# Graph attention on one core: the third attention's row products in two halves around a turned scan, and VectorE's values ahead of the next last maxima

## The chip, the cores and the metric

The kernel runs on 1 core of one Trainium2 chip. The metric is the device time of one execution in microseconds. All times below are from that core. Its engines are named as the profile names them: PE is TensorE (PEld its weight loads), DVE is VectorE, ACT is ScalarE, POOL is GpSimd and SP is SyncE.

## What is computed

Four graph layers run one after the other over 5000 nodes and 85000 edges, which are sorted by destination. Each adds its result to the node features:

```python
h = jnp.maximum(_layernorm(x, axis=-1), 0.0)
x = x + _L0_gnn_ref(h, src, dst, ...)      # mean of the neighbours' rows
h = jnp.maximum(_layernorm(x, axis=-1), 0.0)
x = x + _L1_gnn_ref(h, src, dst, ...)      # relu of two products per edge, mean
h = jnp.maximum(_layernorm(x, axis=-1), 0.0)
x = x + _L2_gnn_ref(h, edge_index, ...)    # two GAT attentions, 16 heads of 8
h = jnp.maximum(_layernorm(x, axis=-1), 0.0)
x = x + _L3_gnn_ref(h, edge_index, ...)    # one dot-product attention, 2 heads of 64
```

The three attentions share one form: a logit for each edge and head, its maximum over the edges of a destination, the exponential of the difference, and a weighted sum of the source rows. In the first two (GAT) the logit is `leaky_relu(al_s[src] + al_d[dst])`. In the third it is the dot product of the destination's query row with the source's key row:

```python
alpha = (q[dst] * k[src]).sum(-1) * (1.0 / np.sqrt(C))
m = jax.ops.segment_max(alpha, dst, num_segments=n)
a = jnp.exp(alpha - m[dst])
denom = jax.ops.segment_sum(a, dst, num_segments=n)
agg = jax.ops.segment_sum(a[:, :, None] * v[src], dst, num_segments=n)
```

## The kernel before

Edges lie in tiles of 128, one edge to a partition. Eight tiles (G = 8) make a group, and 88 groups cover all edges. Five passes sweep over the 88 groups: sum, MLP, GAT, GAT, dot; between them short phases update the nodes. The three attentions are one function, `softmax_pass`, with `kind` "gat" (flag `gat`) or "dot".

In a pass every engine has its own program, and counted semaphores (`eng.wait_ge(*name(p.g))`) join them. A call `turn(p)` stands for one step of an engine's loop, and `p.plus(d)` is the group d further on, so one turn works on several groups at once. The order inside `turn` is the order in which the engine works: it goes through its list strictly, and a wait holds up all that stands behind it.

POOL fetches the source rows of each edge with 8 indirect DMAs a group (L1000) into a ring of 4 slots, `GT`. It may refill a slot when `values` of the group that used it is done. In the dot pass a row has 256 floats (key and value), in the GAT passes 144.

What one turn for group p does in the dot pass, before the change:

- PE: `pe_maxima(p)` (L1313, 24 small products) reads what `dve_lastmax(p)` made; `pe_sums(p-2)` (L1334) adds the weighted rows of each node; `pe_logitT(p+1)` (L1297) turns the logits; `pe_maxedge(p)` (L1321, 24 small products) waits for the running maxima `newM`; `pe_segT(p+1)` (L1303) turns the scanned maxima `seg` back and waits for the scan of DVE; `pe_toedge(p+2)` calls `rows_to_edges` (L1018 to L1024), which takes the destination's query row to each edge: 8 float32 products of 128x128, which the trace shows as 16 passes, into `psD`. They need `Ot32`, which ACT casts in `turn_32`, and a list of 8 block numbers that `loaded` (L185) puts into registers of the engine.
- DVE: `dve_prod(p+1)` (L1346) multiplies `psD` with the key rows; `dve_logit(p+1)` (L1355) sums them; `dve_pen`, `dve_tmax`, `dve_max` make the running maxima (L1378 to L1413); `dve_add(p-2)` (L1436, L1440) adds what `pe_sums` made to `acc`; `dve_segmax(p+1)` (L1362) is the scan over the turned logits; `dve_below(p)` (L1418, L1421) subtracts the maximum; `dve_lastmax(p+1)` (L1370, L1372, L1374) needs `pe_segT(p+1)`; `dve_values(p)` (L1427) weighs the value rows with `factors` and needs ACT's exponential.
- ACT: `act_rescale(p)`; `act_empty(p-1)` (L1269) clears the places that `pe_sums` adds into, and waits for `dve_add(p-2)`; `act_weight(p)` (L1275, L1278) makes the exponentials out of `below`; `act_onehot32(p)` (L1237).

The GAT turn has the same form. Its `dve_prod` is L1343, it has a small `toedge` of 24 bfloat16 products (L1290) in place of the row products, DVE begins with `dve_pen(p)`, and `lastmax`, `newM` and the logits are 8 times as wide.

Of the kernel before, what the change touches and what calls it, by code (L numbers as in the profile page):

```python
# [13 lines left out]
G = 8  # L14
# [51 lines left out]
def program(nc, x, src, dst, w0, b0, w_edge, w_node, b_node, w1, as1, ad1, b1, w2, as2, ad2, b2,  # L66
# [4 lines left out]
    NB = -(-N // P)  # L71
# [23 lines left out]
    with ctx:  # L95
# [20 lines left out]
        blk = sb("blk", [1, SP_], I32)  # L116
# [64 lines left out]
        def loaded(eng, which, table, g, n, most, of=None):  # L181
            if (eng.engine, which) not in reg_sets:
                reg_sets[eng.engine, which] = [eng.alloc_register(f"{which}_{j}") for j in range(n)]
            regs = reg_sets[eng.engine, which]
            eng.load(regs, table[0:1, bass.ds(g * (of or n), n)])  # L185
            return [eng.snap(r, min_val=0, max_val=most) for r in regs]
# [828 lines left out]
            eng.wait_ge(*toedge(p.g - 2))  # L1015
            eng.copy(Ot32[:, p.q, :, :], Ot[:, p.k, :, :]).then_inc(turned32.sem, 1)  # L1016

        def rows_to_edges(eng, p, b):  # L1018

            eng.wait_ge(*turned32(p.g))  # L1020
            eng.wait_ge(*prodded(p.g - 1))
            for j in range(G):
                ins = eng.matmul(psD[:, j, :], Ot32[:, p.q, j, :], at_block(nodeQ, b[j], D), start=True, stop=True)  # L1023
            ins.then_inc(toedge.sem, 1)  # L1024

        def load_hots(eng, p, rows_free, turned_free):

# [176 lines left out]
        def softmax_pass(kind, table, h):  # L1204
            gat = kind == "gat"
# [73 lines left out]


            def pe_toedge(eng, p):
                if not gat:
                    rows_to_edges(eng, p, loaded(eng, "blocks", blk, p.g, G, NB - 1))
                    return
                eng.wait_ge(*staged(p.g))
                eng.wait_ge(*ring_hotT[p.k](p.i))
                eng.wait_ge(*prodded(p.g - 1))
                for j in range(G):
                    for part in range(3):
                        ins = eng.matmul(dst_logits[:, j, :], Ot[:, p.k, j, :], stageD[:, p.q, j, part * h:(part + 1) * h],  # L1290
                                         start=part == 0, stop=part == 2)
                ins.then_inc(toedge.sem, 1)
# [31 lines left out]
            def pe_places(eng, p):  # L1324
                return loaded(eng, "places", blk_off, p.g, G, 2 * BANK + STRIDE)
# [116 lines left out]
            with nc.Block() as block:  # L1442
# [36 lines left out]
                @block.tensor  # L1479
                def _(eng):  # L1480
                    def turn(p):
                        if p.has(-2):
                            off = pe_places(eng, p.plus(-2))
                        if p.has(0):
                            pe_maxima(eng, p)
                        if p.has(-2):
                            pe_sums(eng, p.plus(-2), off)
                        if p.has(1):
                            pe_logitT(eng, p.plus(1))
                        if p.has(0):  # L1490
                            pe_maxedge(eng, p)
                        if p.has(1):
                            pe_segT(eng, p.plus(1))
                        if p.has(2):
                            pe_toedge(eng, p.plus(2))
                    sweep(eng, NG, turn, early=2, late=2)

                @block.vector
                def _(eng):
                    tables_stored(eng)  # L1500
                    eng.memset(lastmax[:, :, :, h:h + 1], 0.0)
                    eng.memset(lastmax1[:, :, :, h:h + 1], 0.0)

                    def turn(p):
                        if gat:
                            if p.has(0):
                                dve_pen(eng, p)
                            if p.has(1):
                                dve_prod(eng, p.plus(1))
                            if p.has(0):  # L1510
                                dve_tmax(eng, p)
                            if p.has(1):
                                dve_logit(eng, p.plus(1))
                            if p.has(0):
                                dve_max(eng, p)
                        else:
                            if p.has(1):
                                dve_prod(eng, p.plus(1))
                                dve_logit(eng, p.plus(1))
                            if p.has(0):  # L1520
                                dve_pen(eng, p)
                                dve_tmax(eng, p)
                                dve_max(eng, p)
                        if p.has(-2):
                            dve_add(eng, p.plus(-2))
                        if p.has(1):
                            dve_segmax(eng, p.plus(1))
                        if p.has(0):
                            dve_below(eng, p)
                        if p.has(1):  # L1530
                            dve_lastmax(eng, p.plus(1))
                        if p.has(0):
                            dve_values(eng, p)
                    sweep(eng, NG, turn, early=2, late=2)
            close((index, onehot32, toedge, prodded, logit, logitT, segmax, segT, flagged, lastmaxed,
                   lastmax1ed, lastmax2ed, nmax, pens, tmaxed, resets, carried, forward, newMed, newM1ed, newM2ed, drop, rescale,
# [46 lines left out]
```

## Time and profile before

| | us |
|---|---|
| median of 3 runs | 5167.67 |
| lowest and highest | 5164.42, 5171.92 |
| the profiled execution | 5178.65 |
| its span in the trace | 5176.9 |

| engine | busy us | share of the span |
|---|---|---|
| PE | 3180.1 | 61% |
| PEld | 2813.0 | 54% |
| DVE | 2733.0 | 53% |
| ACT | 2152.4 | 42% |
| POOL | 3365.2 | 65% |

The profiled execution took 11.0 us more than the median. No engine is busy for more than 65% of the span, so the averages don't tell what bounds the kernel. The passes have to be read one by one: how far apart two turns start, which wait comes in each turn, and what ends it.

### The profile page before, as it was taken

Reading aid. Unit: us, or ns where it says so; the run is one execution under the profiler, and the core shown is the slowest. Engines: PE = TensorE matmul, PEld = TensorE weight load, DVE = VectorE, ACT = ScalarE, POOL = GpSimd, SP = SyncE. Lnnn points to the kernel's source line nnn. Section 1 sums busy time; section 2 is a strip of 40 time slices with the busy share of each in tenths; the row PEclk is TensorE's granted clock in tenths of the full one; section 3 lists DMA queues with packets and bytes.
Section 4 is the critical chain, followed back from the end, with each engine's and each line's share of the span. In section 5 each row is a group of like instructions: output and inputs, shape, how many; then the busy total and the mean of one; then the engine's idle time right before and its main releaser. Section 6 shows DMA issues by size and latency. Waiting matters only on the chain. (4 is left out here: it accounts for less than half of the span.)

```text
span 5176.9 us, 111400 instructions
## 1 busy us (share of the span) xinstructions
PE 3180.1 (61%) x29524; PEld 2813.0 (54%) x29525; DVE 2733.0 (53%) x6724; ACT 2152.4 (42%) x6586; POOL 3365.2 (65%) x3551
## 2 busy tenths in 40 slices
PE   1555555566666665666666646666665566666664
PEld 0444444455655654565656536566564466666664
DVE  4222222332222225677777767777777666666666
ACT  2222222243333325666666556666664333333332
POOL 1777777557777772777777537777773366666662
PEclk9766666687777777656666656665666777676766
DMA  4333333233333332444444224444441344444442
GB/s 125 106 105 105 105 105 104 80 101 105 105 105 105 105 97 60 115 117 118 117 113 117 78 83 118 117 113 118 117 117 54 111 141 134 133 132 135 134 133 74
DMA packets 331553, 563.97 MB, mean 109 GB/s; under 512 B 79101, under 2 KB 149773, under 8 KB 331438
## 3 DMA queue, kind: packets, MB, share of 16 engines
q0 software_dynamic: 124288, 289.37, 21.2%
q1 hardware_dynamic: 207170, 273.48, 16.3%
q8 instruction: 42, 0.69, 0.1%
q14 instruction: 53, 0.43, 0.0%
HBM read 490.38 MB, written 72.84 MB: 109 GB/s over the span
## 5 line engine op out<-in xcount | busy, mean ns | idle before, releaser
L1000 POOL DMA_INDIRECT GT<-table,srcI x3520 | 3351.0, 952 | 1688.0 <-issue 1055.0
L1334 PE MATMUL psA<-V,O 128*128 128x144 f32 (+1 forms) x4224 | 932.8, 403 | 17.4 <-ACT psA L1269 14.9
L1334 PEld LDWEIGHTS psA<-V,O 128*128 128x128 f32 x4224 | 864.8, 294 | 24.0 <-issue 18.7
L1023 PE MATMUL psD<-nodeQ,Ot 128*128 x2816 | 608.0, 403 | 386.9 <-ACT Ot L1016 298.8
L1023 PEld LDWEIGHTS psD<-nodeQ,Ot 128*128 128x128 f32 x2816 | 561.6, 305 | 416.0 <-issue 416.0
L1055 DVE TENSOR_TENSOR acc<-acc,psA 128x1032 f32 (+1 forms) x176 | 215.1, 1222 | 703.6 <-PE psA L1134 673.9
L1269 ACT COPY psA<-consts 128x1296 f32<-128x1296 f32 (+1 forms) x264 | 318.6, 1207 | 368.0 <-DVE acc L1440 368.0
L1180 DVE TENSOR_TENSOR prod<-psD,GT 128x1024 f32<-128x1024 f32 x88 | 107.7, 1224 | 667.1 <-DMA GT<-table,srcI 667.1
L1046 PE MATMUL psA<-zerob 1*128 1x258 bf16 (+1 forms) x704 | 164.5, 378 | 414.1 <-issue 329.1
L1258 ACT COPY nodeM<-newM 128x16 f32 x1408 | 307.7, 219 | 259.2 <-ACT nodeM L1258 230.3
L1440 DVE TENSOR_TENSOR acc<-acc,psA 128x1296 f32 (+1 forms) x264 | 385.6, 1461 | 55.4 <-PE psA L1334 26.2
L1303 PE MATMUL psT<-ident,seg 128*128 128x128 f32 (+1 forms) x264 | 95.7, 362 | 470.1 <-DVE seg L1362 470.1
L1010 ACT COPY srcI<-srcT 128x8 int32 (+1 forms) x440 | 84.3, 193 | 689.3 <-DMA GT<-table,srcI 682.1
L1263 ACT ACTIVATE resc<-diff 128x16 f32<-128x16 f32 (+1 forms) x264 | 55.9, 212 | 733.5 <-DVE acc L1436 687.6
L1165 ACT ACTIVATE V<-prod 128x1024 f32<-128x1024 f32 x88 | 93.0, 1057 | 616.4 <-DVE prod L1180 616.4
L1321 PEld LDWEIGHTS psS<-newM,Ot 128*128 128x128 bf16 x6336 | 189.3, 99 | 290.8 <-DVE newM L1413 288.9
L1321 PE MATMUL psS<-newM,Ot 128*128 128x16 bf16 (+1 forms) x6336 | 211.3, 174 | 212.8 <-DVE newM L1413 212.5
L1134 PE MATMUL psA<-GT,O 128*128 128x129 f32 x1408 | 329.8, 427 | 0.0
L1134 PEld LDWEIGHTS psA<-GT,O 128*128 128x128 f32 x1408 | 305.9, 329 | 36.6 <-issue 36.6
L1046 PEld LDWEIGHTS psA<-zerob 1*128 1x128 bf16 x704 | 68.7, 118 | 470.5 <-issue 447.6
L1427 DVE TENSOR_TENSOR V<-GT,psA 128x1024 f32<-128x1024 f32 x264 | 320.8, 1215 | 3.7 <-ACT psA L1275 3.4
L1303 PEld LDWEIGHTS psT<-ident,seg 128*128 128x128 f32 (+1 forms) x264 | 43.4, 164 | 492.1 <-DVE seg L1362 323.0
(221 smaller groups left out, 5304.1 us busy)
## 6 DMA issues: line engine op xcount, KB each, us to landing
Ob<-onehots SPq DMA_DIRECT2D x352, 256.0 KB
Ot<-onehots_turned SPq DMA_DIRECT2D x352, 256.0 KB
GT<-table,srcI POOLq DMA_INDIRECT x3520
onehots<-Ob SPq DMA_DIRECT2D x88, 256.0 KB
onehots_turned<-Ot SPq DMA_DIRECT2D x88, 256.0 KB
first<-first_dram SPq DMA_DIRECT2D x176, 64.0 KB
first_dram<-GT SPq DMA_DIRECT2D x18, 384.0 KB, 5.1
table<-GT SPq DMA_DIRECT2D x40, 144.0 KB, 1.9
```

What stands on the lines that cost most here:

```text
L1000: eng.indirect_dma_start(out=GT[:, p.k, j, 0:table.shape[1]], out_offset=None, in_=table, in_offset=bass.IndirectOffsetOnAxis(ap=srcI[:, p ...
L1023: ins = eng.matmul(psD[:, j, :], Ot32[:, p.q, j, :], at_block(nodeQ, b[j], D), start=True, stop=True)
L1046: eng.matmul(psA[:, a:a + 2, 0:w], zerob[0:1, 0:P], zerob[0:1, 0:2 * w], start=True, stop=False, skip_group_check=True)
L1055: eng.tensor_tensor(a, a, psA[:, :, 0:w], ALU.add).then_inc(added.sem, 1)
L1134: ins = eng.matmul(to, O[:, p.q, j, :], GT[:, p.k, j, 0:w], start=False, stop=j == G - 1, skip_group_check=True)
L1258: eng.copy(at_block(nodeM, b[j], h), by_step(newM[:, p.q, 0:HG])[:, :, j]).then_inc(noted.sem, 1)
L1269: eng.copy(places, consts[:, 0:1, :].unsqueeze(1).to_broadcast([P, 3, 3, VW])).then_inc(emptied.sem, 1)
L1303: eng.transpose(segR, seg[0:HG, p.q, :], ident[0:HG, 0:HG]).then_inc(segT.sem, 1)
L1321: ins = eng.matmul(edge_max[:, j, :], Ot[:, p.k, j, :], part, start=n == 0, stop=n == 2)
L1334: ins = eng.matmul(flatA[:, bass.ds(off[j], VW)], O[:, p.q, j, :], V[:, p.q, j, 0:VW], start=False, stop=j == G - 1, skip_group_check=True)
L1427: eng.tensor_tensor(v[:, :, :, 0:C], heads(GT[:, p.k, :, f0:f0 + D], h), wide(factors, C), ALU.mult)\
L1440: eng.tensor_tensor(to, to, places, ALU.add).then_inc(added.sem, 1)
```

## The change

Two things change, both in the order of one engine's work, and no instruction of computation is added or removed.

In the dot pass alone, PE issues the 8 products of `rows_to_edges` in two halves of 4, one before `pe_segT` and one behind it. The registers with the block numbers are loaded at the start of the turn. In all three attentions, DVE does `dve_values(p)` before `dve_lastmax(p+1)`.

```diff
-        def rows_to_edges(eng, p, b):
-
-            eng.wait_ge(*turned32(p.g))
-            eng.wait_ge(*prodded(p.g - 1))
-            for j in range(G):
+        def rows_to_edges(eng, p, b, half=None):
+
+            if not half:
+                eng.wait_ge(*turned32(p.g))
+                eng.wait_ge(*prodded(p.g - 1))
+            for j in range(G) if half is None else range(half * G // 2, (half + 1) * G // 2):
                 ins = eng.matmul(psD[:, j, :], Ot32[:, p.q, j, :], at_block(nodeQ, b[j], D), start=True, stop=True)
-            ins.then_inc(toedge.sem, 1)
+            if half != 0:
+                ins.then_inc(toedge.sem, 1)
...
                     def turn(p):
                         if p.has(-2):
                             off = pe_places(eng, p.plus(-2))
+                        if not gat and p.has(2):
+                            b = loaded(eng, "blocks", blk, p.g + 2, G, NB - 1)
                         if p.has(0):
                             pe_maxima(eng, p)
...
                             pe_maxedge(eng, p)
+                        if not gat and p.has(2):
+                            rows_to_edges(eng, p.plus(2), b, 0)
                         if p.has(1):
                             pe_segT(eng, p.plus(1))
                         if p.has(2):
-                            pe_toedge(eng, p.plus(2))
+                            if gat:
+                                pe_toedge(eng, p.plus(2))
+                            else:
+                                rows_to_edges(eng, p.plus(2), b, 1)
...
                         if p.has(0):
                             dve_below(eng, p)
+                            dve_values(eng, p)
                         if p.has(1):
                             dve_lastmax(eng, p.plus(1))
-                        if p.has(0):
-                            dve_values(eng, p)
```

PE in the loop of the dot pass, before: from the last product of `pe_maxedge` (L1321) over the turned scan (L1303) and the load of the block numbers (L185) to the row products (L1023).

```order
L1321 MATMUL psS<-newM,Ot 128x2 x24
L1303 MATMUL psT<-ident,seg 128x16
L185 ISA
L185 TENSOR_LOAD blk
L186 ISA
L1021 REGISTER_ALU
L1023 ISA
L1023 MATMUL psD<-nodeQ,Ot 128x128
L1023 ISA
L1023 MATMUL psD<-nodeQ,Ot 128x128
```

The same place after, where L1320 is `pe_maxedge`, L1302 the turned scan and L1024 the row products:

```order
L1320 MATMUL psS<-newM,Ot 128x2 x24
L1021 REGISTER_ALU
L1022 REGISTER_ALU
L1024 ISA
L1024 MATMUL psD<-nodeQ,Ot 128x128
L1024 ISA
L1024 MATMUL psD<-nodeQ,Ot 128x128
L1024 ISA
L1024 MATMUL psD<-nodeQ,Ot 128x128
L1024 ISA
L1024 MATMUL psD<-nodeQ,Ot 128x128
L1302 MATMUL psT<-ident,seg 128x16
```

Four row products now stand ahead of the turned scan, and the load of `blk` is gone from between the scan and the rest of them.

PE at the border of two turns after the change, from the second half's last product to the next `pe_maxima` (L1312):

```order
L1024 MATMUL psD<-nodeQ,Ot 128x128
L185 ISA
L185 TENSOR_LOAD blk_off
L186 ISA
L185 ISA
L185 TENSOR_LOAD blk
L186 ISA
L1312 MATMUL psS<-lastmax,Ob 128x3 x24
```

The load of `blk` now follows that of `blk_off`, which alone stood here before.

DVE in the loop of the GAT passes, before: `dve_below` (L1418, L1421), the three steps of `dve_lastmax`, then `dve_values` (L1427).

```order
L1418 TENSOR_TENSOR below<-lg,psS 128x128 [waits weight,maxedge]
L1421 TENSOR_SCALAR below<-below 128x128 [waits belowed]
L1370 ISA [waits nmax,segT]
L1370 TENSOR_TENSOR lastmax<-psT,lastT 128x8x16
L1372 TENSOR_TENSOR lastmax<-lastmax 128x8x16 [waits lastmaxed]
L1374 TENSOR_TENSOR lastmax<-lastmax 128x8x16 [waits lastmax1ed]
L1427 TENSOR_TENSOR V<-GT,psA 128x128x8 [waits sums,factor]
```

The same place after, one line number lower:

```order
L1417 TENSOR_TENSOR below<-lg,psS 128x128 [waits weight,maxedge]
L1420 TENSOR_SCALAR below<-below 128x128 [waits belowed]
L1426 TENSOR_TENSOR V<-GT,psA 128x128x8 [waits sums,factor]
L1369 ISA [waits nmax,segT]
L1369 TENSOR_TENSOR lastmax<-psT,lastT 128x8x16
L1371 TENSOR_TENSOR lastmax<-lastmax 128x8x16 [waits lastmaxed]
L1373 TENSOR_TENSOR lastmax<-lastmax 128x8x16 [waits lastmax1ed]
```

The values with their wait for ACT's factors now stand directly behind `below`, and the last maxima come behind them. The dot pass has the same move.

## Rows read from the trace of the kernel before

**Rows 1.** Windows inside a GAT and the dot pass: busy time of each engine.

```profile
core 0: us, PE busy (x) PEld busy (x) DVE busy (x) ACT busy (x) POOL busy (x), PEclk, DMA share, GB/s
...
2100.00:2920.00 820.00, 552.12 (x7290) 499.61 (x7290) 592.59 (x1537) 520.84 (x2019) 622.80 (x648) 0.64 0.42 117
...
4110.00:5110.00 1000.00, 667.54 (x6914) 621.71 (x6914) 646.20 (x1610) 326.62 (x840) 642.51 (x678) 0.73 0.44 133
```

**Rows 2.** First and last start of the logits' first step: dot, then first GAT.

```profile
L1346 DVE TENSOR_TENSOR prod<-psD,GT x88: 1223/1225/1225, 4088.9 to 5114.6; 128x1024 f32<-128x1024 f32 x88
...
L1343 DVE TENSOR_TENSOR lg<-psD,GT x88: 290/291/293, 2056.9 to 2939.1; 128x128 f32<-128x128 f32 x88
```

**Rows 3.** Waits of the dot pass, 4110:5110, total, times, longest.

```profile
DVE prod L1346 <- PE psD L1023: 238.6, 84, 3.0
...
POOL GT L1000 <- DVE V L1427: 149.7, 72, 2.4
...
PE psD L1023 <- issue: 85.9, 84, 1.1
```

**Rows 4.** Timeline of one turn of the dot pass: start, duration, engine, line.

```profile
4658.86 0.26 PE L1303 MATMUL psT<-ident,seg 16*128 16x16 f32 x1 [1.95 <-DVE seg L1362]
...
4660.14 3.78 PE L1023 MATMUL psD<-nodeQ,Ot 128*128 x16 [1.03 <-issue]
...
4663.71 0.83 PE L1313 MATMUL psS<-lastmax,Ob 128*128 128x3 bf16 x24
4663.96 1.22 DVE L1346 TENSOR_TENSOR prod<-psD,GT 128x1024 f32<-128x1024 f32 x1 [2.94 <-PE psD L1023]
...
4668.19 0.76 PE L1321 MATMUL psS<-newM,Ot 128*128 128x2 bf16 x24 [1.04 <-DVE newM L1413]
...
4669.11 1.37 DVE L1440 TENSOR_TENSOR acc<-acc,psA 128x1170 f32 x1
...
4670.95 0.20 PE L1303 MATMUL psT<-ident,seg 16*128 16x16 f32 x1 [2.00 <-DVE seg L1362]
4671.31 0.18 DVE L1370 TENSOR_TENSOR lastmax<-psT,lastT 128x16 f32<-128x16 f32 x1 [0.23 <-PE psT L1303]
...
4671.67 0.18 ACT L1275 ACTIVATE psA<-below 128x16 f32<-128x16 f32 x1
4671.74 0.19 DVE L1374 TENSOR_TENSOR lastmax<-lastmax 128x16 bf16<-128x16 f32 x1
```

**Rows 5.** The fetches by line, in a GAT and in the dot window.

```profile
L1000 POOL DMA_INDIRECT GT<-table,srcI x648 | 623.3, 962 | 197.5 <-issue 193.5 <-DVE V L1427 4.0
...
L1000 POOL DMA_INDIRECT GT<-table,srcI x678 | 642.5, 948 | 346.9 <-issue 197.3 <-DVE V L1427 149.7
```

**Rows 6.** Windows for line 1334 (`pe_sums`) alone, GAT and dot: PE busy.

```profile
2100.00:2920.00 820.00, 326.72 (x1296) 303.47 (x1296) 0.64 0.42 117
...
4110.00:5110.00 1000.00, 211.63 (x1344) 194.93 (x1344) 0.73 0.44 133
```

**Rows 7.** Timeline of one turn of the first GAT pass.

```profile
2620.29 0.29 DVE L1370 TENSOR_TENSOR lastmax<-psT,lastT 128x128 f32<-128x128 f32 x1 [0.21 <-PE psT L1303]
...
2620.94 0.29 DVE L1374 TENSOR_TENSOR lastmax<-lastmax 128x128 bf16<-128x128 f32 x1
2621.15 1.21 DVE L1427 TENSOR_TENSOR V<-GT,psA 128x1024 f32<-128x1024 f32 x1
...
2621.49 0.79 PE L1313 MATMUL psS<-lastmax,Ob 128*128 128x17 bf16 x24 [0.72 <-DVE lastmax L1374]
...
2622.13 4.19 PE L1334 MATMUL psA<-V,O 128*128 128x144 f32 x16
...
2624.24 0.29 DVE L1343 TENSOR_TENSOR lg<-psD,GT 128x128 f32<-128x128 f32 x1 [1.76 <-DMA GT<-table,srcI]
...
2627.79 1.50 DVE L1440 TENSOR_TENSOR acc<-acc,psA 128x1296 f32 x1
...
2630.59 0.28 ACT L1275 ACTIVATE psA<-below 128x128 f32<-128x128 f32 x1
```

More of the change, by code:

```diff
@@ L1281, in pe_toedge @@
             def pe_toedge(eng, p):
-                if not gat:
-                    rows_to_edges(eng, p, loaded(eng, "blocks", blk, p.g, G, NB - 1))
-                    return
                 eng.wait_ge(*staged(p.g))
```

## The prediction, made before the changed kernel had run

> **What bounds the kernel now.** I start from the windows of single passes, since the page's shares mix passes with different limits. No engine is full in either of them [rows 1]: in the dot window PE is busy 668 of 1000 us, DVE 646, POOL 643. So each pass is bounded by a cycle of waits or by an issue rate. The starts of one instruction give the length of a turn. In the dot pass 88 of them lie between 4088.9 and 5114.6, which is 1025.7 / 87 = 11.79 us a turn; in the GAT pass it is 882.2 / 87 = 10.14 us [rows 2].
>
> Next the waits, and what ends them. In the dot pass DVE waits once a turn for the row products (238.6 us in 84 turns, 2.84 each), and POOL waits for DVE's values (149.7 us) [rows 3]. So POOL runs ahead until its ring is full, and the pass hangs on a cycle between PE and DVE. One turn shows it [rows 4]: the turned scan starts at 4658.86, the row products follow at 4660.14 after 1.03 us of "issue", they last 3.78 us, and only then `prod` starts (4663.96). From `prod` to the next turned scan it is 4670.95 - 4663.96 = 6.99 us, DVE's own work nearly throughout. The cycle is 1.28 + 3.82 + 6.99 = 12.09 us in this turn, a long one, and has no slack. PE itself stands idle for 2.00 us before the turned scan (1.95 in the turn before) [rows 4].
>
> The GAT passes are different. There DVE's first step waits for the fetched rows (1.76 us in the turn shown [rows 7]), and POOL issues without a stop: its busy time and its gaps make 623.3 + 197.5 = 820.8 us of a window of 820 [rows 1, 5], 81 turns of 10.13 us. POOL's issue is the floor of that pass, and DVE's 1.76 us are the slack that the change may use up.
>
> **Part 1: the row products in two halves.** The first half now lies in PE's idle 2.00 us before the turned scan. Half of 3.78 us is 1.89 us, and the stretch from the end of `maxedge` (4668.19 + 0.76 = 4668.95) to the turned scan (4670.95) is 2.00 us long [rows 4]. It fits with nothing over. What the half waits for (`turned32`, `prodded` of the group before) was done turns or microseconds earlier: that `prod` ended at 4665.18 [rows 4]. The 1.03 us of issue after the turned scan are the load of the block numbers: 85.9 us in 84 turns, the only thing that stands between [rows 3]. It moves behind the second half, next to the load that is already there, where PE has queued products to work on. So from the turned scan to `prod` remain about 0.25 us for the scan itself and 1.89 us for the second half, with 0.04 to 0.1 us of hand-over: 2.2 us where 5.10 stood (4663.96 - 4658.86) [rows 4]. That takes 2.9 us out of PE's side of the cycle, as much as the whole wait of `prod`. The moved load can cost between 0, if it is hidden, and its 1.03 us; I take 0, because today the neighbouring load costs no gap there (the row products end at 4663.92, and `maxima` starts at 4663.71, in their tail) [rows 4].
>
> What is late next? First DVE's own list. `prod` to `add` is 4669.11 - 4663.96 = 5.15 us. `add` to factors, through ACT's clearing, is 4671.67 - 4669.11 = 2.56 us, 0.18 for the factors and some 0.04 to the values. The last maxima take 4671.74 + 0.19 - 4671.31 = 0.62 us [rows 4], and the values 1.21 (from the GAT turn, the same shape [rows 7]). Sum: 5.15 + 2.56 + 0.22 + 1.21 + 0.62 = 9.76 us, and some 0.2 less where neighbours overlap: 9.5 to 9.8. Second, PE's own list: maxima 0.8, sums 211.63 / 84 = 2.52 us in the mean and up to the GAT pass's 4.19 at the lower clock [rows 6, 7], `maxedge` 0.8, two halves of 1.9, turned scan 0.25 and the turned logits about as much: 8.4 to 10.1 us with everything back to back. Third, POOL: 8 fetches of 0.948 us, each with its gap of issue. Over all 678 fetches the gap is 197.3 / 678 = 0.29 us, over the 606 that it is put down to 0.33: 9.91 to 10.19 us a turn; the GAT row's 10.13 lies between [rows 5]. **POOL is the largest**, and I take the middle, 10.05 us. The dot pass then becomes bounded by issue, like the GAT passes: 87 x (11.79 - 10.05) = **151 us saved**, between 139 (at 10.19) and 164 (at 9.91).
>
> **Part 2: values ahead of the last maxima, dot pass.** Before, the last maxima filled the time in which ACT made the factors: the factors are ready at 4671.67 + 0.18 = 4671.85, the maxima end at 4671.93 [rows 4]. The values can start at most 0.1 us earlier, and the last maxima come 1.2 us later. That delay sits inside the 9.5 to 9.8 us above, and is hidden by POOL's 10.05. Cost 0; without that cover it would be 0 to 0.6 us a turn.
>
> **Part 3: the same move in the two GAT passes.** Here there is no gain to have: POOL's issue is the floor. There is a cost, if a longer cycle passes 10.13 us. I follow it [rows 7]. The values start when the factors are ready: `add` starts at 2627.79, factors end at 2630.59 + 0.28 = 2630.87, which makes 3.08 + 0.04 = 3.12 us. The values take 1.21, less 0.08 of overlap. The last maxima take 0.94 us (2620.29 to 2621.23). Then PE: the maxima start 2621.49 - 2621.23 = 0.26 us behind them, and the sums 0.64 later. The sums take 4.19 us in this turn, 326.72 / 81 = 4.03 in the mean [rows 6]. Then `add` can start, 0.05 us on. Sum: 3.12 + 1.13 + 0.94 + 0.26 + 0.64 + 4.03 + 0.05 = 10.17 us, and up to 10.3 if the two hand-overs that I set at 0.05 are longer. Before, the 1.13 us of the values stood outside this cycle. Now it passes POOL's floor by 0.04 to 0.17 us. I take 0.12: 174 turns x 0.12 = **21 us lost**, between 0 and about 50: with sums of 4.19 us each time and 0.1 more of hand-over the cycle is 10.42 us, and (10.42 - 10.13) x 174 = 50.
>
> **Sum.** 151 - 21 = 130 us. The profiled execution of 5178.65 us would become about 5049. It lies 11.0 us above the median of the runs, and the changed passes are repeated turns that should not differ between executions, so the forecast is 5167.7 - 130 = **5038 us**. Its own range is 5015 to 5060.
>
> **What the clock may do.** The mean of the sums, 4.03 us, is near the 4.19 of the turn shown, so most of them already run at the lower level and little is left to lose [rows 6, 7]. In the GAT window the granted clock is 0.64 in the mean [rows 1], between the levels of 1.2 and 2.4 GHz, and the sums take 4.03 us in the mean where the dot pass, at 0.73, does almost as many columns in 2.52 [rows 1, 6]. The change widens PE's pause between the small products behind the turned scan and the maxima, from 0.72 us by the values and the maxima (1.13 + 0.94) to some 2.7 us [rows 7]. The Trainium skill (TensorE: Matmul & The Clock Gate, section HAM oscillation — how this bites in real kernels) says that idle gaps between bursts of products bring the clock down and that each burst then starts slow. The trace agrees in its direction, since the sums behind a pause are slow today; by the rule all of them would then be so, and the sum would be 5067.
>
> **Rivals.** (a) The move costs the GAT passes nothing: the cycle stays under 10.13 us, since PE's products lie closer together behind the pause, the clock rises within them, and the sums take less than 3.99 us. Then 5167.7 - 151 = 5017. For it speaks that the sum is within 0.2 us of the floor; against, that the mean of the sums is 4.03.
> (b) All sums of the GAT passes at the lower level: 50 us lost there, 5167.7 - 151 + 50 = 5067. For it speaks that 4.19 us is already close to the mean, and that the pause before the burst grows from 0.72 to 2.7 us. The rule cited above would give the same.
> (c) PE remains the limit of the dot pass. If products run at the lower level and the two loads of registers (1.03 us each) are hidden by neither half, PE's list is up to 10.1 + 2.1 = 12.2 us. At 10.9, where it is 10.1 + 0.8, 77 us are saved and 21 lost: 5112. Against it speaks that one such load is hidden completely now.
> (d) Slower: the same mechanism in full. The place is PE between the second half and the next maxima, the price both loads unhidden, 2.1 us, behind last maxima that come 1.2 us later than today. It decides where PE's list plus loads exceeds 11.79 us; at 12.0 the dot pass loses 0.2 x 87 = 18 us and the GAT passes 21 to 50: 5207 to 5236. For it speaks only that nothing in the trace shows two loads in a row.
>
> **How the numbers follow.** Forecast 0.60, (a) 0.14, (b) 0.13, (c) 0.10, (d) 0.03. The range from 5010 to 5100 leaves out (d) and the slower half of (c), and its lower end takes a floor of 9.96 us with no loss in the GAT passes, 5167.7 - 159 = 5009. A measurement of this kernel tells about 0.2%, 10 us, from no change. All cases but (d) are faster by more; 0.02 goes to no difference.
>
> **What would show it.** Right: turns of the dot pass 10.0 to 10.15 us apart; `prod` there waits for the fetched rows and no longer for `psD`; POOL no longer waits for the values; no wait of PE for `seg`, or one of a few tenths; in the GAT passes turns of 10.2 to 10.3 us, `add` waiting for the sums, and POOL beginning to wait for the values. Wrong: an issue gap before the maxima in the dot pass, or sums in the GAT passes that are clearly shorter or longer than 4.0 us.

## The result and the profile after the change

The changed kernel takes 5047.28 us (median of four runs, 5046.14 to 5048.22); the kernel before, on the same chip, 5167.77 (5164.42 to 5171.92). The ratio is 0.9766, 95% interval 0.9749 to 0.9783: 120 us less. The range and the direction held; the forecast of 5038 was 9 us too low. The two profiled executions differ by 5178.65 - 5048.22 = 130.4 us, where the sum was 130; that these two agree so well is partly luck, as the last part on the prediction shows.

First the length of the passes. These are the groups of the logits' first step in the changed kernel: the dot pass, then both GAT passes, with mean duration, then first and last start.

```profile
L1345 DVE TENSOR_TENSOR prod<-psD,GT x88: 1224/1225/1227, 4107.0 to 4983.1; 128x1024 f32<-128x1024 f32 x88
...
L1342 DVE TENSOR_TENSOR lg<-psD,GT x88: 287/292/293, 2053.9 to 2945.6; 128x128 f32<-128x128 f32 x88
...
L1342 DVE TENSOR_TENSOR lg<-psD,GT x88: 289/292/293, 3064.7 to 3955.9; 128x128 f32<-128x128 f32 x88
```

| pass | turn before, us | turn after, us | whole pass |
|---|---|---|---|
| first GAT | 10.140 | 10.249 | 9.5 longer |
| second GAT | 10.138 | 10.244 | 9.1 longer |
| dot | 11.790 | 10.070 | 149.6 shorter |

A turn is last start less first start, by 87. The account closes: the dot pass starts 4107.0 - 4088.9 = 18.1 us later [rows 2] and its last turn starts 131.5 us earlier.

The waits of the dot pass (window 4110 to 4970; in total, how often, longest) answer to [rows 3]:

```profile
POOL GT L1000 <- issue: 207.8, 682, 0.3
...
PE psS L1312 <- DVE lastmax L1373: 81.7, 62, 1.7
DVE V L1426 <- ACT psA L1277: 67.2, 85, 0.8
...
DVE prod L1345 <- DMA GT<-table,srcI: 50.5, 82, 4.4
PE psT L1302 <- DVE seg L1361: 48.9, 62, 1.0
```

DVE's `prod` no longer waits for the row products, 2.84 us a turn before [rows 3], but 0.6 us for fetched rows. POOL's wait for the values is gone, and what stays is its own gap of issue, 0.30 us each. The wait of PE for `seg` has fallen from about 2 us to 0.6 a turn, since the first half of the row products stands there. PE's issue gap ahead of the row products is gone too. At the load's new place, ahead of the maxima (L1312), the wait is put down to DVE's last maxima, 1.3 us each in 62 turns. The maxima start 0.25 us behind the last maxima in most turns (median, 0.36 in the mean), as they do in the GAT pass, which has no load of `blk`. So most of the loads' time lies under that wait here. In the timeline of one turn (start, duration, engine, line) both halves can be seen, as the two pieces of L1024:

```profile
4587.72 1.22 DVE L1426 TENSOR_TENSOR V<-GT,psA 128x1024 f32<-128x1024 f32 x1 [0.81 <-ACT psA L1277]
...
4589.27 0.19 DVE L1373 TENSOR_TENSOR lastmax<-lastmax 128x16 bf16<-128x16 f32 x1
...
4589.71 0.75 PE L1312 MATMUL psS<-lastmax,Ob 128*128 128x3 bf16 x24 [1.64 <-DVE lastmax L1373]
...
4590.10 1.23 DVE L1345 TENSOR_TENSOR prod<-psD,GT 128x1024 f32<-128x1024 f32 x1 [0.64 <-DMA GT<-table,srcI]
...
4594.18 0.78 PE L1320 MATMUL psS<-newM,Ot 128*128 128x2 bf16 x24 [0.43 <-DVE newM L1412]
...
4594.81 1.14 PE L1024 MATMUL psD<-nodeQ,Ot 128*128 x8
...
4596.88 0.20 PE L1302 MATMUL psT<-ident,seg 16*128 16x16 f32 x1 [0.93 <-DVE seg L1361]
4597.03 1.15 PE L1024 MATMUL psD<-nodeQ,Ot 128*128 x8
```

Compare [rows 4]: one piece of 3.78 us began 1.28 us after the turned scan and ended in `prod`'s start; now the second half ends at 4598.18, long before the next `prod`. DVE's own gap has moved to the values, which wait 0.8 us for the factors: in the order of before, the last maxima filled it.

The GAT passes show the other side. Waits in 2100 to 2920, then one turn:

```profile
PE psS L1312 <- DVE lastmax L1373: 198.9, 80, 2.6
...
DVE pen L1377 <- PE psS L1312: 78.0, 72, 1.1
DVE V L1426 <- ACT psA L1277: 64.1, 79, 0.8
...
DVE acc L1439 <- PE psA L1333: 25.8, 74, 0.7
...
POOL GT L1000 <- DVE V L1426: 7.6, 25, 0.3
```

```profile
2645.44 1.22 DVE L1426 TENSOR_TENSOR V<-GT,psA 128x1024 f32<-128x1024 f32 x1 [0.83 <-ACT psA L1277]
...
2647.22 0.29 DVE L1373 TENSOR_TENSOR lastmax<-lastmax 128x128 bf16<-128x128 f32 x1
...
2647.76 0.79 PE L1312 MATMUL psS<-lastmax,Ob 128*128 128x17 bf16 x24 [2.49 <-DVE lastmax L1373]
2648.48 4.07 PE L1333 MATMUL psA<-V,O 128*128 128x144 f32 x16
...
2652.59 1.50 DVE L1439 TENSOR_TENSOR acc<-acc,psA 128x1296 f32 x1 [0.41 <-PE psA L1333]
...
2654.20 1.24 ACT L1271 COPY psA<-consts 128x1296 f32<-128x1296 f32 x1 [1.71 <-DVE acc L1439]
...
2655.38 0.27 ACT L1277 ACTIVATE psA<-below 128x128 f32<-128x128 f32 x1
...
2655.69 1.22 DVE L1426 TENSOR_TENSOR V<-GT,psA 128x1024 f32<-128x1024 f32 x1 [0.83 <-ACT psA L1277]
```

Values to values is 10.25 us, and every step on the way waits for the one before: factors, values, last maxima, maxima, sums, `add`, clearing, factors. In this ring no step has slack. PE now stands idle 2.49 us ahead of the maxima, where it was 0.72 [rows 7]. The first step of the logits has no wait in this window that would rank beside these; before it had 1.76 us in the turn shown [rows 7].

### The profile page after: what moved, and what is told of

The parts are those of the page before. It is cut to its first block and busy times, and to the rows that moved or that the text cites. A ratio compares the mean times of both kernels' runs of the same rounds, so it can differ in the third digit from the quotient of the medians.

```text
span 5046.5 us, 111480 instructions
## 1 busy us (share of the span) xinstructions
PE 3128.2 (62%) x29524; PEld 2797.0 (55%) x29525; DVE 2725.9 (54%) x6724; ACT 2151.6 (43%) x6586; POOL 3355.3 (66%) x3551
## 3 DMA queue, kind: packets, MB, share of 16 engines
q0 software_dynamic: 124288, 289.37, 21.6%
## 5 line engine op out<-in xcount | busy, mean ns | idle before, releaser
L1333 PE MATMUL psA<-V,O 128*128 128x144 f32 (+1 forms) x4224 | 1002.0, 426 | 17.5 <-ACT psA L1271 14.9
L1333 PEld LDWEIGHTS psA<-V,O 128*128 128x128 f32 x4224 | 939.9, 317 | 24.0 <-issue 18.5
L1024 PE MATMUL psD<-nodeQ,Ot 128*128 x2816 | 544.2, 363 | 291.7 <-ACT Ot L1016 291.7
L1024 PEld LDWEIGHTS psD<-nodeQ,Ot 128*128 128x128 f32 x2816 | 485.6, 265 | 316.2 <-issue 313.0
L1312 PE MATMUL psS<-lastmax,Ob 128*128 128x17 bf16 (+1 forms) x6336 | 207.8, 173 | 552.9 <-DVE lastmax L1373 522.1
L1312 PEld LDWEIGHTS psS<-lastmax,Ob 128*128 128x128 bf16 x6336 | 189.0, 103 | 582.9 <-issue 582.8
L1239 ACT CAST O<-Ob 128x1024 f32<-128x1024 bf16 x264 | 273.8, 1037 | 0.0
L1199 PE MATMUL psA<-V,O 128*128 128x128 f32 x1408 | 254.8, 355 | 0.0
```

The lines of the kernel that those rows point to most:

```text
L1199: ins = eng.matmul(to, O[:, p.q, j, :], V[:, p.q, j, 0:D], start=False, stop=j == G - 1, skip_group_check=True)
L1239: eng.copy(O[:, p.q, :, :], Ob[:, p.k, :, :]).then_inc(onehot32.sem, 1)
L1312: ins = eng.matmul(maxima[:, j, :], Ob[:, p.k, j, :], part, start=n == 0, stop=n == 2)
L1333: ins = eng.matmul(flatA[:, bass.ds(off[j], VW)], O[:, p.q, j, :], V[:, p.q, j, 0:VW], start=False, stop=j == G - 1, skip_group_check=True)
```

## Experiments

Each kernel was timed beside the kernel before on its chip. Unless said otherwise its edit starts from the changed kernel.

**Halves only.** All values go back behind the last maxima; the two halves and the early load stay.

```diff
                         if p.has(0):
                             dve_below(eng, p)
-                            dve_values(eng, p)
                         if p.has(1):
                             dve_lastmax(eng, p.plus(1))
+                        if p.has(0):
+                            dve_values(eng, p)
```

> The changed kernel with the values back behind the last maxima in all three attentions; only the halves of the row products and the early load remain. My theory: the dot pass stays at the rate of POOL's fetches (10.07 us a turn), and the GAT passes fall back from 10.25 to 10.14 us, so 18 to 19 us less than the changed kernel's 5047: 5029. Rival: the halves bring their gain only because the values come first (the last maxima would wait for the turned scan with the values queued behind them). Then the dot pass is slower than 10.07 us a turn, by up to 0.6, and the time is 5047 or above.

Measured: 5020.53 us (5018.82 to 5022.27) against 5169.26, ratio 0.9711 (0.9695 to 0.9728). With the third kernel below this is the fastest, 27 us below the change. The expectation of 5029 was 8.5 us too high, since it counted only the turns. Its GAT turn is back at 10.12, its dot turn is that of the change:

```profile
L1345 DVE TENSOR_TENSOR prod<-psD,GT x88: 1223/1225/1226, 4081.8 to 4957.8; 128x1024 f32<-128x1024 f32 x88
...
L1342 DVE TENSOR_TENSOR lg<-psD,GT x88: 290/292/293, 2054.2 to 2935.0; 128x128 f32<-128x128 f32 x88
```

One row of its waits in the dot pass (4110 to 4950) tells about the load. The last maxima come earlier here, and what stands ahead of PE's maxima is now a gap of issue, 0.95 us in 64 turns:

```profile
PE psS L1312 <- issue: 60.7, 64, 1.8
```

So the loads are not hidden in PE's list, as I had assumed, once the last maxima come early. The gap can't be put down to the moved load alone, since two loads now stand in a row there. Nobody waits for it: in this window `prod` waits for fetched rows in 83 turns (87.0 us) and never for row products, since PE has slack under POOL's floor.

The dot pass starts 25.2 us earlier than in the change and is as long (876.0 and 876.1). So the whole difference lies ahead of it: 21.6 us in the turns of the two GAT passes, the rest between passes.

**Values only.** The kernel before, with nothing but the values moved, in all three passes.

> The kernel before with only the values moved ahead of the last maxima. My theory: nothing in the dot pass (the last maxima end 2 us before the row products do), and 0.11 us a turn lost in the GAT passes, so 18 us slower than before: 5186, with GAT turns of 10.25 us. Rival: the GAT passes' slower turns have to do with the other half of the change; then 5168.

Measured: 5193.98 us (5192.90 to 5196.63), ratio 1.0050 (1.0033 to 1.0067). The move alone makes the kernel 25 us slower, 8 us more than the 5186 expected from the turns. Its first GAT pass and its dot pass:

```profile
L1343 DVE TENSOR_TENSOR lg<-psD,GT x88: 285/291/293, 2053.9 to 2943.4; 128x128 f32<-128x128 f32 x88
...
L1346 DVE TENSOR_TENSOR prod<-psD,GT x88: 1223/1224/1225, 4104.8 to 5127.8; 128x1024 f32<-128x1024 f32 x88
```

GAT turns of 10.224 and 10.244, a dot turn of 11.758 where it was 11.790. Even where PE bounds the dot pass the order of the values matters to it by 0.03 us a turn, 3 us.

**Values ahead in the dot pass alone**, with halves and early load.

```diff
                             dve_below(eng, p)
-                            dve_values(eng, p)
+                            if not gat:
+                                dve_values(eng, p)
                         if p.has(1):
                             dve_lastmax(eng, p.plus(1))
+                        if p.has(0) and gat:
+                            dve_values(eng, p)
```

> The changed kernel with the values ahead of the last maxima in the dot pass alone. My theory: the same 5029 as with the halves alone, since POOL's fetches set the turn of the dot pass with either order. Rival: the order of the values is worth something in the dot pass; then it is below the kernel with the halves alone by some 5 us or more.

Measured: 5020.63 us (5019.71 to 5023.14), ratio 0.9712 (0.9696 to 0.9728), dot turn 10.058: the same as halves only. In the dot pass the order is worth nothing that can be measured, under POOL's floor as above it.

**Early load only.** The kernel before with the load moved to the start of the turn; the row products stay in one piece behind the turned scan.

```diff
+                        if not gat and p.has(2):
+                            b = loaded(eng, "blocks", blk, p.g + 2, G, NB - 1)
                         if p.has(0):
                             pe_maxima(eng, p)
...
                         if p.has(2):
-                            pe_toedge(eng, p.plus(2))
+                            if gat:
+                                pe_toedge(eng, p.plus(2))
+                            else:
+                                rows_to_edges(eng, p.plus(2), b)
```

> The kernel before with only the load of the block numbers moved to the start of the turn in the dot pass; the 8 row products stay in one piece behind the turned scan. My theory: the 1.02 us of issue after the turned scan go, the cycle of PE and DVE gets as much shorter, turns of 10.77 us in place of 11.79: 89 us less, 5079. Rival: the gain of the change is that of the halves alone, and the load was covered or comes back as a gap before the maxima; then 5168 or a little less.

Measured: 5037.73 us (5034.38 to 5047.64), ratio 0.9744 (0.9727 to 0.9760). A miss by 41 us: I expected the load's own 1.03 us a turn. The pass:

```profile
L1346 DVE TENSOR_TENSOR prod<-psD,GT x88: 1223/1224/1226, 4081.2 to 4983.2; 128x1024 f32<-128x1024 f32 x88
```

902.0 / 87 = 10.37 us a turn, 1.42 less than before. This profiled execution was the longest of the four (5047.64), so its turn is on the long side, and still at least 0.39 us a turn came from elsewhere than the load's 1.03. The windows for the row products' line alone show from where; first the kernel before in its dot pass, then this one (start and end, length, PE busy and products, weight loads, granted clock, DMA share, GB/s):

```profile
4110.00:5110.00 1000.00, 311.41 (x1344) 288.13 (x1344) 0.73 0.44 133
```

```profile
4110.00:4970.00 860.00, 257.25 (x1317) 234.59 (x1316) 0.70 0.51 153
```

Per turn of 16 products that is 311.41 / 84 = 3.71 us before and 257.25 / 82.3 = 3.13 now. The products themselves are the same. The sums (L1334), for which DVE waits 3.1 us in all of this window, went the other way in the same window:

```profile
4110.00:4970.00 860.00, 275.42 (x1328) 254.57 (x1328) 0.70 0.51 153
```

That is 275.42 / 83 = 3.32 us a turn where it was 211.63 / 84 = 2.52 [rows 6], and the granted clock of the whole pass is 0.70 against 0.73. So PE did not run faster over the pass. Slow stretches went from the row products, on which `prod` waits, to the sums. Single turns of this kernel stand at either end:

```profile
4581.78 1.84 PE L1023 MATMUL psD<-nodeQ,Ot 128*128 x15
...
4590.80 3.56 PE L1023 MATMUL psD<-nodeQ,Ot 128*128 x15
```

The view cuts one product off each time: 15 of them in 1.84 or 3.56 us, almost 1:2, as the two levels of 2.4 and 1.2 GHz are. All 16 take 2.05 to 3.78 us in this pass. Before, nearly all turns had the slow form (3.71 in the mean, never under 3.18); here more stand nearer to the fast one. With the gap of issue gone, the row products follow the turned scan sooner, 0.34 us behind its start in the mean where it was 1.26. That this is what lets them run at the upper level is an argument and not shown; that they take less time is. What still bounds this kernel is PE: `prod` waits 1.3 us a turn for the row products, and PE 1.6 us for `seg`.

```profile
PE psT L1303 <- DVE seg L1362: 127.5, 82, 2.0
...
DVE prod L1346 <- PE psD L1023: 109.3, 81, 2.0
```

The halves take this rest away, but only a part of it can be had before POOL's floor: by the medians 5037.73 - 5020.53 = 17 us, 0.20 us a turn, and by the two traces 902.0 - 876.0 = 26 us, 0.30 a turn.

**Exponentials ahead of the clearing.** In the changed kernel ACT clears `psA` (1.24 us) ahead of the factors, and the factors' exponentials come behind. Here the weights' step of ACT goes in front of it.

```diff
+                        if p.has(0):
+                            act_weight(eng, p)
...
-                            act_weight(eng, p)
```

> The changed kernel with one more move, on ACT: the exponentials for group p (L1277, L1280) stand ahead of the clearing of the places (L1271) in each turn of the three attentions. It takes the clearing, 1.24 us, out of the cycle of the GAT passes (add, clearing, factors, values, last maxima, maxima, sums, add). My theory: the factors start when below is done, 2.3 us behind the start of add in place of 2.8, the cycle is 0.45 us shorter and falls under POOL's floor; GAT turns of 10.12 us again, 5047 - 26 = 5021, while the dot pass stays at 10.07. Rival: the clearing isn't on the cycle, or the sums then wait for it; then the GAT turns stay at 10.24 or grow.

Measured: 5029.37 us (5027.77 to 5029.49) against 5170.51, ratio 0.9726: 18 us below the change. The GAT turns are 10.130 and 10.123, POOL's floor, and the logits wait for fetched rows again:

```profile
L1342 DVE TENSOR_TENSOR lg<-psD,GT x88: 289/292/293, 2053.8 to 2935.1; 128x128 f32<-128x128 f32 x88
```

```profile
DVE lg L1342 <- DMA GT<-table,srcI: 34.8, 79, 1.0
```

A step taken off the ring on ACT undoes the loss, with the values still ahead. So the loss was the ring's, as Part 3 had it, and not the place of the values as such. Its dot pass starts 4087.9, which is 6 us behind halves only and makes up most of the 9 us left between them; I did not trace those.

**Half of the fetches.** To see the other limits POOL's floor has to go. This kernel is the change with half of the fetches, so it leaves half of the source rows out of the result; the semaphore's count is halved with them, and the unused half of each slot holds zeros.

```diff
-                for j in range(G):
+                for j in range(G // 2):
```

> The changed kernel with only 4 of the 8 fetches of each group in all passes (half of the source rows left out of the result), on another chip than the first time. POOL's floor falls to about 5 us a turn. My theory: the GAT passes stay at 10.24 us a turn, since the cycle through the sums sets them and not POOL; the dot pass goes to 9.5 to 9.8 us, DVE's own list; the fetches save 87 x 0.4 = 35 us there and about 220 in the sum and MLP passes. Rival: GAT turns below 10.1.

Measured: 4258.35 us in one run. The passes, the first GAT pass once in the window 1500 to 2200 and once whole:

```profile
L1342 DVE TENSOR_TENSOR lg<-psD,GT x69: 289/292/293, 1501.1 to 2197.2; 128x128 f32<-128x128 f32 x69
...
L1342 DVE TENSOR_TENSOR lg<-psD,GT x88: 287/292/293, 1336.5 to 2217.7; 128x128 f32<-128x128 f32 x88
...
L1345 DVE TENSOR_TENSOR prod<-psD,GT x88: 1219/1225/1226, 3363.4 to 4192.0; 128x1024 f32<-128x1024 f32 x88
```

```profile
POOL GT L1000 <- DVE V L1426: 373.8, 69, 5.6
```

Inside the GAT pass (window 1500 to 2200) 68 turns take 696.1 us, 10.24 each, within 0.01 us of what they take with all fetches, while POOL stands idle 5.4 us of each. The whole pass has a mean of 10.13, since its first ten turns are only 9.24 us apart and all later ones some 10.24. So in the changed kernel the ring bounds the GAT passes from about the tenth turn on, and POOL doesn't. In the dot pass, where the change has left POOL as the bound, the turn falls to 828.6 / 87 = 9.52 us: DVE's list with its wait for ACT's factors, which the prediction put at 9.5 to 9.8. Of the expectation the part on the sum and MLP passes missed: the first GAT pass starts 717 us earlier (1336.5 against 2053.9) where about 220 were expected, so those passes hung on the fetches far more than I thought. I did not trace them.

**Whole ahead, and halves of fetches, on other chips.** Four kernels asked whether the row products can stand in one piece ahead of the turned scan, so that no half is needed.

```diff
                         if not gat and p.has(2):
-                            rows_to_edges(eng, p.plus(2), b, 0)
+                            rows_to_edges(eng, p.plus(2), b)
                         if p.has(1):
                             pe_segT(eng, p.plus(1))
                         if p.has(2):
                             if gat:
                                 pe_toedge(eng, p.plus(2))
-                            else:
-                                rows_to_edges(eng, p.plus(2), b, 1)
```

> The changed kernel with all 8 row products ahead of the turned scan in the dot pass, not 4. The turned scan then starts at about 7.3 + 3.6 = 10.9 us after the values in place of 9.1, and the last maxima behind it. My theory: DVE does the values meanwhile (10.1 to 11.3 on that scale), so the last maxima end at 11.9 to 12.1, 0.3 us later than in the changed kernel, which the wait for POOL's fetches covers: 5047 to 5055. Rival: the turned scan is on the path even with the values ahead of it; then the turn grows by up to 1.8 us and the time goes to 5100 or more.

> All 8 row products ahead of the turned scan, and the values behind the last maxima in all attentions as before the change. My theory: here the values wait for the last maxima, and these for the turned scan at 10.9 on the scale of the turn: values at 11.7 where 10.07 is the floor. The dot pass loses 1.0 to 1.7 us a turn against the kernel with the halves alone (5020.5), so 5110 to 5165; this is the cover that the order of the values gives. Rival: DVE has room enough, and the time stays within 10 us of 5020.5.

> The changed kernel with only 4 of the 8 fetches of each group, in all passes; the other half of each ring slot holds zeros, so half of the source rows are left out of the result. POOL's floor falls to about 5 us a turn and what is next shows. My theory: the GAT passes stay at 10.24 us a turn, since the cycle through the sums sets them, and the dot pass goes to 9.5 to 9.8 us, DVE's own list. Rival: the GAT passes were still bounded by POOL and its hand-overs, and go below 10.1.

> The kernel before with only 4 of the 8 fetches of each group, in all passes (half of the source rows left out of the result). My theory: the dot pass stays at 11.8 us a turn, since PE and DVE set it, and the GAT passes fall by the 1.7 us for which DVE waited for the rows, from 10.14 to about 8.5 us a turn. Rival: something else than the fetches holds the GAT turns near 10.1, and they stay.

These four shared a chip on which the kernel before itself took 6844.35 us, 32% more than elsewhere. Measured: 7620.06 us (ratio 1.1138, 1.1122 to 1.1154) with the values ahead, 6758.38 (0.9881, 0.9867 to 0.9895) with the values last, and for the half fetches 5400.48 after and 4669.35 before, one run each. The first two were run again on another chip:

> All 8 row products ahead of the turned scan in the dot pass, the values ahead of the last maxima, on another chip than the first time. My theory, as before: the turned scan starts 1.8 us later, DVE does the values meanwhile, the last maxima end 0.3 us later than in the changed kernel, which the wait for POOL's fetches covers: 5047 to 5055, so that the halves themselves bring nothing that the early load and the order of the values don't. Rival: the turn grows by up to 1.8 us, and the time goes to 5100 or more.

> The same with the values behind the last maxima, on the same chip. My theory: the values wait for the last maxima and these for the turned scan, so the dot pass loses 1.0 us a turn or more against the kernel with the halves alone (5020.5): 5110 or above. Rival: DVE has room enough, and the time stays within 10 us of 5020.5.

Once more the chip had the kernel before at 6898.93 us, and they came out alike: 7750.65 (1.1235, 1.1216 to 1.1253) and 6811.49 (0.9880, 0.9863 to 0.9896). The GAT code of the kernel with values ahead is that of the change, line for line, and its GAT turn was 19.20 us here instead of 10.24. One place in its trace stands out, PE's maxima and the step of DVE that reads them. The first and the last of POOL's eight fetches of the group stand beside it:

```profile
3006.54 0.95 POOL L1000 DMA_INDIRECT GT<-table,srcI  x1 [4.48 <-DVE V L1426]
...
3006.76 0.81 PE L1312 MATMUL psS<-lastmax,Ob 128*128 128x17 bf16 x24 [3.14 <-DVE lastmax L1373]
...
3015.29 0.95 POOL L1000 DMA_INDIRECT GT<-table,srcI  x1 [0.31 <-issue]
3017.93 0.17 DVE L1377 TENSOR_SCALAR pen<-psS 128x8 f32<-128x8 f32 x1 [11.40 <-remote]
```

```profile
DVE pen L1377 <- remote: 723.0, 67, 11.4
```

The maxima end at 3007.57, and `pen` starts 10.4 us later; in the change's trace it starts 0.04 us later, and POOL goes on fetching meanwhile. The wait is booked as coming from outside the traced engines, in 67 turns of the window 2600 to 4100. What fills the time is POOL's list: its eight fetches end at 3016.24, and `pen` starts 1.7 us behind them. With four fetches a group, on the same chip, the delay is half as long, 4.8 us behind the maxima (median), and `pen` again starts about a microsecond behind the last fetch:

```profile
2302.04 0.95 POOL L1000 DMA_INDIRECT GT<-table,srcI  x1 [0.31 <-issue]
...
2304.08 0.17 DVE L1377 TENSOR_SCALAR pen<-psS 128x8 f32<-128x8 f32 x1 [5.80 <-remote]
```

With the values last it is another step of DVE that waits for PE, `below`, and it too starts 1.8 to 1.9 us (medians) behind POOL's last fetch. So on these two chips a wait of DVE for PE tends to end only when POOL's group of fetches is done. Why it does there and not on the others no run shows.

The runs also show which order suffers more. With the values ahead, this delay lies in the same ring as the sums and the values, and the GAT turn is 19.2 and 19.9 us on the two chips; with the values last it is 15.1 and 15.3. With half of the fetches, on the first of these chips, it is 14.4 for the change and 9.4 to 9.5 for the kernel before, while the dot turn is 11.29 for the change and 13.05 for the kernel before. None of the six expectations above was met, and they can't be judged by these chips, since they reckoned with the turns of the others. The question that the runs were for, whether one piece ahead of the scan does as well as two halves, stays open: no such kernel ran on a chip like the others.

## Why the prediction was right, and where it was not

**Dot pass: right.** Turn 10.070 us where 10.05 was taken (9.91 to 10.19), 149.6 us saved where it said 151. The floor is POOL's issue: its waits hold nothing but 0.30 us of gap at each fetch, and with half of them the turn falls to 9.52. DVE's list with the wait for ACT, 9.5 to 9.8, fits the same run. Part 2, at 0 us, was right by two comparisons: 0.1 us between values ahead and values last in the dot pass, and 0.03 us a turn above the floor.

**The split within Part 1: wrong, and without effect on the sum.** The step took 1.03 us for the load and 1.89 for the half, 2.9 together, with row products of constant duration. By the traces the load alone brought 1.42 us a turn, since the row products fell from 3.71 to 3.13 us with it, and the halves the remaining 0.30. By medians 131.5 of 148.7 us came from the load and 17 from the halves. The sum did not feel it, because it went by the floor of 10.05 and not by the 2.9 us taken out. In the early-load kernel, where the floor is not reached, the error was in the open: 41 us. The step failed where it took a duration from before for work whose duration changes once its neighbour moves.

**Part 3: right in mechanism and nearly in size.** It forecast 0.12 us a turn; it was 0.109 and 0.106. The mean turn, measured from the start of the values: 1.14 to the last maxima, 0.94 for these, 0.25 to the maxima, 0.70 to the sums, 4.07 for the sums, 0.04 to `add`, and 3.10 through the clearing and the factors. Together 10.24, where the working had 10.17 and took 10.25. The half fetches show that this ring and not POOL sets the turn, and the earlier exponentials that its ACT part counts. What it missed is the stretch between passes: 18.6 us of loss are turns, and the whole cost of the move is 24.7 us over the kernel before and 26.8 over halves only. The start and the end of a pass are not in "174 turns".

**The clock, rival (b): did not happen.** In the same window the sums take

```profile
2100.00:2920.00 820.00, 326.31 (x1280) 308.17 (x1280) 0.67 0.42 116
```

326.31 / 80 = 4.08 us against 4.03 [rows 6], and the granted clock is 0.67 against 0.64. PE's pause grew from 0.72 to 2.5 us and the sums hardly noticed. The sums were slow already, as the prediction said, so there was little left to lose. The rule named there from the Trainium skill (TensorE: Matmul & The Clock Gate, section HAM oscillation — how this bites in real kernels) is not contradicted by this, since the bursts do start slow; but a wider pause cost 0.05 us a turn and not the 50 us of the rival. Rival (a), no loss at all, failed by the same row: the sums didn't fall under 3.99. (c) and (d) fell in part for another reason than the one that I gave. I held that the loads would be hidden. In the changed kernel most of their time is, but under the wait for the last maxima and not behind products; halves only shows a gap of 0.95 us before the maxima, which the prediction had named as a sign that it is wrong. PE's list with the loads still stays under 10.07 us, in a pass where row products and sums run faster than the 1.9 us a half and the 4.19 us that (c) reckoned with: halves of 1.46 us (251.69 us for 1375 products in 4110 to 4970) and sums of 3.2 in the mean. The five chances and the 0.02 for no difference add up to 1.02, a slip.

**The last 9 us: the level from which the sum was taken.** The sum of 130 is that of the two profiled executions. I then took it off the median, on the ground that the changed passes should not differ between executions, so that the 11.0 us between the profiled run and the median would be in both kernels. They were not: the change's profiled run, 5048.22, is within 1 us of its median. Of the 11 us some 7 lie ahead of the dot pass: three kernels with the same code up to there (halves only, values ahead in the dot pass alone, early load) reach it at 4081.8, 4081.8 and 4081.2, and the profiled run of before at 4088.9 [rows 2], with GAT turns of 10.140 against 10.125. The profiled run of before was a long one there, by 0.015 us a turn and a few microseconds between passes. Counted by the experiments' medians the move of the values cost about 26 us, where the sum had 21, and the dot pass gave 149, where it had 151. That is 123 us, against 120 measured, so the sum of 130 was 10 us too large, and the 130.4 between the two profiled executions met it by luck. Where the other 4 us of the 11 lay stays open, since only one trace of the kernel before was used.

## What to carry to other kernels

Before reordering one pass for the sake of another, follow each ring of waits through the new order and compare its sum with the pass's floor: here the same line of code was free in one pass and cost 0.11 us a turn in two others, and leaving it out of them is 27 us faster (5020.6 us). A gap of issue ahead of a burst of products is worth removing first, alone. Here a gap of 1.03 us brought 1.42 us a turn, since the burst behind it got shorter too, while the slower products fell to sums for which hardly anything waited (3.1 us in the pass's window). No run shows what it brings in a pass that waits for both. When a floor caps the gain, cost the edit against the floor, and try its parts singly, cheapest first: one moved load gave 88% of what load and halves gave together.

## What was not expected of the hardware

The same 15 row products took 1.84 or 3.56 us in neighbouring turns of one pass, and the mean of a turn's 16 moved from 3.71 to 3.13 us when a 1.03 us gap ahead of them went, with the sums of the same turns going from 2.52 to 3.32. A duration of PE read from the trace is therefore that of its order, too.

POOL's issue keeps the same rate whether rows are those of the GAT passes or of the dot pass: 962 and 948 ns and 0.3 us of gap [rows 5], 10.06 to 10.13 us for eight fetches in the GAT and dot passes of every kernel that reached it on these chips.

On two of the four chips used for the experiments the kernel before took 6844 and 6899 us, and in the changed order DVE's wait for PE's maxima lasted 10.4 us longer than the products, in turn after turn, and ended 1 to 2 us behind POOL's last fetch of the group; with four fetches in place of eight it lasted 4.8 us longer. The ranking of versions changed with it: with the row products whole ahead, the order with values ahead lost 11 to 12% there. The cause stays open.
